# Gated MLP with ternary weights on one core: the total of |down_w| moves from TensorE to two small DMAs and VectorE, and the first eviction moves ahead of the last weights' low parts

## The reference

```python
scale = cond @ norm_w.T + 1.0
ms = jnp.mean(x * x, axis=-1, keepdims=True)
h = x * (scale[:, None, :] * jax.lax.rsqrt(ms + EPS))
u = h @ up_w.T
val, gate = jnp.split(u, 2, axis=-1)
h = val * jax.nn.gelu(gate, approximate=False)
hq = act_quant(h)
wq = weight_quant(down_w)
y = hq @ wq.T
return y + x
```

```python
scale = 1.0 / jnp.clip(jnp.mean(jnp.abs(w)), 1e-05, None)
return jnp.clip(jnp.round(w * scale), -1.0, 1.0) / scale
```

## Time and profile before

| | us |
|---|---|
| median of 3 runs | 426.77 |
| lowest, highest | 426.59, 426.85 |
| the profiled execution's own time | 426.46 |
| its span | 424.7 |
| TensorE busy in the span | 420.3 (99%) |
| VectorE busy | 279.4 (66%) |
| ScalarE busy | 187.9 (44%) |
| GpSimd busy | 165.2 (39%) |
| granted TensorE clock, mean | 1.000 |

### The profile page before, as it was taken

The page is one execution under the profiler, slowest core; times in us unless marked ns, Lnnn a source line. Parts: engine busy times, 40 slices in busy tenths (PEclk is TensorE's granted clock), DMA queues, the critical chain, the costliest instruction groups (busy, mean ns, idle before and its releaser), DMA issues.

```text
span 424.7 us, 7679 instructions
## 1 busy us (share of the span) xinstructions
PE 420.3 (99%) x2089; PEld 337.4 (79%) x2089; DVE 279.4 (66%) x538; ACT 187.9 (44%) x335; POOL 165.2 (39%) x323
## 2 busy tenths in 40 slices
PE   8999999999999999999999999999999999999997
PEld 6778888888888788888888887888888888878786
DVE  4986656756657657567566576565675565765676
ACT  6764344444344443444443444434444434444541
POOL 2644443443434434434424344334344243343320
PEclk9999999999999999999999999999999999999999
DMA  8523444333443424443334434244433344342324
GB/s 271 203 54 111 115 99 121 101 79 94 123 99 99 115 71 111 99 121 102 80 93 124 99 100 119 67 109 99 123 99 78 95 124 99 100 120 68 83 51 125
DMA packets 82088, 45.01 MB, mean 106 GB/s; under 512 B 68256, under 2 KB 68768, under 8 KB 81952
## 3 DMA queue, kind: packets, MB, share of 16 engines
q1 hardware_dynamic: 81792, 44.60, 40.3%
q10 hardware_dynamic: 288, 0.33, 0.3%
HBM read 20.00 MB, written 8.39 MB: 67 GB/s over the span
## 4 chain that ended last, share of the span: by engine, by line
PE 96%; DMA 1%; DVE 1%; ACT 1%; SPq 0%; issue 0%; POOL 0%; DVEq 0%; POOLq 0%
PE p_gate L768 41%; PE p_val L768 41%; PE p_y L788 13%; DMA up_raw<-up_w_t 1%; DVE up_lo L487 0%; PE p_val L746 0%; ACT up_hi L376 0%; DVE y_sb L531 0%; PE p_val L752 0%; PE p_val L747 0%; PE p_gate L788 0%; SPq L223 0%; ACT gelu L386 0%; DVE h L496 0%; DVE y_sb L668 0%
## 5 line engine op out<-in xcount | busy, mean ns | idle before, releaser
L625 DVE SCALAR_TENSOR_TENSOR h<-p_val,rstd,gelu 128x512 f32<-128x512 f32 x124 | 92.4, 745 | 128.0 <-PE p_val L768 127.1
L426 ACT ACTIVATE gelu<-p_gate,rstd 128x512 f32<-128x512 f32 x124 | 84.9, 685 | 142.7 <-PE p_gate L768 135.6
L299 POOL TENSOR_TENSOR mean_sq_eps<-mean_sq,rms_eps 128x1 f32<-128x1 f32 x64 | 12.2, 190 | 234.2 <-ACT squares L360 234.2
L372 ACT ACTIVATE q<-q_rounded 128x1024 bf16<-128x1024 f32 x63 | 66.6, 1057 | 77.9 <-DVE q_rounded L592 77.9
L768 PE MATMUL p_gate<-up_hi,a_lo 128*128 128x512 f32 x248 | 80.6, 406 | 0.0
L768 PE MATMUL p_val<-up_hi,a_hi 128*128 128x512 f32 x248 | 78.2, 396 | 0.0
L768 PE MATMUL p_val<-up_hi,a_lo 128*128 128x512 f32 x248 | 78.1, 396 | 0.0
L768 PE MATMUL p_val<-up_lo,a_hi 128*128 128x512 f32 x248 | 78.1, 396 | 0.0
L768 PE MATMUL p_gate<-up_hi,a_hi 128*128 128x512 f32 x248 | 78.1, 396 | 0.0
L768 PE MATMUL p_gate<-up_lo,a_hi 128*128 128x512 f32 x248 | 78.1, 395 | 0.0
L578 DVE TENSOR_REDUCE h_max<-h 128x1 f32<-128x1024 f32 x63 | 76.5, 1215 | 1.2
(11 more groups left out here) (87 smaller groups left out, 250.0 us busy)
## 6 DMA issues: line engine op xcount, KB each, us to landing
xt_in<-x_t SPq DMA_DIRECT2D x32, 256.0 KB, 2.8
x_all<-x SPq DMA_DIRECT2D x32, 256.0 KB, 2.9
out<-y_sb SPq DMA_DIRECT2D x31, 256.0 KB, 2.0
up_raw<-up_w_t SPq DMA_DIRECT2D x7, 256.0 KB, 5.3
down_raw<-down_w_t SPq DMA_DIRECT2D x1, 1024.0 KB, 7.9
q_t<-q SPq DMA_TRANSPOSE x63, 3.1
up_raw<-up_w_t ACTq DMA_DIRECT2D x1, 256.0 KB, 2.9
out<-y_sb SPq DMA_DIRECT2D x1, 128.0 KB, 2.0
```

The costliest lines, as they stand in the source:

```text
L299: pool.tensor_tensor(mean_sq_eps[:, j:j + 1], mean_sq[:, j:j + 1], rms_eps[:, :], ALU.add).then_inc(pool_step, 1)
L372: act.activation(q[j % 2][:, :], q_rounded[j % 2][:, :], ACT.Copy, bias=-ROUND).then_inc(q_ready, 1)
L426: act.activation(gelu[c][:, :], p_gate[c][:, :], ACT.Gelu, scale=rstd[:, j:j + 1]).then_inc(gelu_done, 1)
L625: nc.vector.scalar_tensor_tensor(h[s][:, c * W:(c + 1) * W], p_val[c][:, :], rstd[:, j:j + 1], gelu[c][:, :], op0=ALU.mult, op1=ALU.mult). ...
```

## The change

- The 128 sums of `abs_sum` go by a DMA into one row of one partition (`sums_row`). SyncE issues it in front of its first transpose, when ScalarE has the sums.
- VectorE adds that row up on one partition (`total`), makes a row of 128 copies times 1/(FF*D) out of it, and clips it from below (`mean_row`). These three instructions stand between the quantising of tile 0 and the last early eviction, `early_h(1, 1)`, and begin with a wait for the DMA.
- A second DMA, also ahead of SyncE's first transpose, spreads the row over the 128 partitions of `mean_abs`.
- TensorE's product with the ones goes, and so does VectorE's L504, which read its result. `ternary(0)` waits for the second DMA in its place.
- `early_h(0, 0)` on VectorE moves ahead of `low_part(3, 0)`, and `high_part(2, 1)` on ScalarE ahead of `early_gelu(0, 0)`.

```diff
+            sp.wait_ge(abs_ready, 1)
+            sp.dma_start(sums_row[0:1, :], abs_sum[:, 0:1]).then_inc(sums_in_row, 16)
+
+            sp.wait_ge(mean_in_row, 3)
+            sp.dma_start(mean_abs[:, 0:1], mean_row[0:1, :]).then_inc(mean_landed, 16)
...
             high_part(2, 0)
+            high_part(2, 1)
             early_gelu(0, 0)
-            high_part(2, 1)
             high_part(3, 0)
...
-                        act.wait_ge(ternary_step, 4)
+                        act.wait_ge(ternary_step, 3)
...
-                    dve.wait_ge(total_done, 1)
-                    nc.vector.tensor_scalar(mean_abs[:, :], p_y[1][:, 0:1], 1.0 / (FF * D), CLIP,
-                                            ALU.mult, ALU.max).then_inc(ternary_step, 1)
+                    dve.wait_ge(mean_landed, 16)
+                    nc.vector.reciprocal(down_scale[:, :], mean_abs[:, :]).then_inc(ternary_step, 1)
...
             low_part(2, 1)
+            early_h(0, 0)
             low_part(3, 0)
-            early_h(0, 0)
             low_part(3, 1)
             early_h(1, 0)
             early_h(0, 1)
             quantised(0, 0, 0)
+            dve.wait_ge(sums_in_row, 16)
+            nc.vector.tensor_reduce(total[:, :], sums_row[:, :], axis=AX.X, op=ALU.add).then_inc(mean_in_row, 1)
+
+            dve.wait_ge(consts_ready, 1)
+            dve.wait_ge(mean_in_row, 1)
+            nc.vector.tensor_scalar(mean_row[:, :], ones[0:1, :], total[:, 0:1], 1.0 / (FF * D),
+                                    ALU.mult, ALU.mult).then_inc(mean_in_row, 1)
+
+            dve.wait_ge(mean_in_row, 2)
+            nc.vector.tensor_scalar(mean_row[:, :], mean_row[:, :], CLIP, None, ALU.max).then_inc(mean_in_row, 1)
             early_h(1, 1)
             quantised(0, 1, 1)
...
-                    if first and j == TPB:
-
-                        pe.wait_ge(consts_ready, 1)
-                        pe.wait_ge(abs_ready, 1)
-                        nc.tensor.matmul(p_y[1][:, 0:1], ones[:, :], abs_sum[:, :], start=True,
-                                         stop=True).then_inc(total_done, 1)
```

More of the change, by code:

```diff
@@ L76, in build @@
         down_scale = sb("down_scale", [P, 1], fp32)
+        sums_row = sb("sums_row", [1, P], fp32)
+        mean_row = sb("mean_row", [1, P], fp32)
+        total = sb("total", [1, 1], fp32)
         x_all = sb("x_all", [P, B, TPB, D], fp32)
@@ L139, in build @@
         abs_ready = sem("abs_ready")
-        total_done = sem("total_done")
+        sums_in_row = sem("sums_in_row")
+        mean_in_row = sem("mean_in_row")
+        mean_landed = sem("mean_landed")
         ternary_step = sem("ternary_step")
@@ L501, in ternary @@
                 if stage == 0:
-                    dve.wait_ge(total_done, 1)
-                    nc.vector.tensor_scalar(mean_abs[:, :], p_y[1][:, 0:1], 1.0 / (FF * D), CLIP,
-                                            ALU.mult, ALU.max).then_inc(ternary_step, 1)
+                    dve.wait_ge(mean_landed, 16)
+                    nc.vector.reciprocal(down_scale[:, :], mean_abs[:, :]).then_inc(ternary_step, 1)
                     dve.wait_ge(ternary_step, 1)
-                    nc.vector.reciprocal(down_scale[:, :], mean_abs[:, :]).then_inc(ternary_step, 1)
-                    dve.wait_ge(ternary_step, 2)
                     nc.vector.tensor_scalar(down_tmp[:, :, :], down_raw[:, :, :], down_scale[:, 0:1], ROUND,
@@ L513, in ternary @@
                 if stage == 1:
-                    dve.wait_ge(ternary_step, 3)
+                    dve.wait_ge(ternary_step, 2)
                     nc.vector.tensor_scalar(down_tmp[:, :, :], down_tmp[:, :, :], ROUND + 1.0, ROUND - 1.0,
```

## The result

| | before | changed |
|---|---|---|
| median of 8 runs, us | 426.64 | 428.18 |
| lowest, highest | 426.57, 426.85 | 427.84, 428.40 |
| span of the profiled execution | 424.7 | 426.4 |

The ratio is 1.0034, with a 95% interval of 1.0024 to 1.0043: the change makes the kernel slower by 1.5 us. The forecast was 427.4 with a range of 426.5 to 428.2, so the time lies just inside. The sign and the place are those of the forecast; the size is not: 1.54 us came where 0.58 was summed. In the forecast's own chances the change was to stay within 0.2% with 0.68, and to be slower by more with 0.28; the less likely of the two came.

A forecast was written before the change was run, and what follows sets the result against it. TensorE, busy 99%, was taken to bound the kernel; tile 4's wait for the late gelu adds L - 0.75 - 0.35 - 0.12 = +0.58 us to 426.77, giving 427.4, range 426.5 to 428.2.

The forecast's parts named there:

- L: First DMA's time from issue to landing, taken as 1.8 us; TensorE's first product of tile 4 moves by L - 1.22.
- The early gain: TensorE up to 0.62 us earlier, from the first eviction's stall and the dropped ones product; forecast as swallowed at tile 4.
- With 0.03 each between them 0.88: VectorE's reduction, product and clip on one partition behind the first DMA: 0.28, 0.28 and 0.23 plus hops, 0.88 us.
- A rival of the prediction: The gain stands: tile 3's gelu not late, as when VectorE's later steps run faster; 426.15 to 426.7, chance 0.15.
- the slack of 0.35: Before tile 4, the margin between the end of tile 3's gelu and TensorE's weight load: 28.29 - 27.94 us.
- the credit of 0.12: At tile 4, a stopped TensorE restarts quicker: 0.34 us from freed load to second product, against 0.46 in the flow.
- The line through the two loads: A line through the 80 KB and 256 KB load times, giving 1.5 us for a DMA of no bytes.
- The rival of a slow transfer: First DMA slow: at L = 2.07 the kernel is 0.85 us slower, at L = 3.1 +1.9; chance 0.27.
- The reordering's 0.41: TensorE's stall of 0.41 us at the first eviction, waiting for the first early_h; the reordering was to remove it.
- some 0.1 of the gain is lost: If the last low part on VectorE takes as long as the slower of its kind, 0.35 us more.
- Costed at nothing: Second DMA, SyncE's first transpose, other evictions and tile 4's x: all forecast early enough to add no time.
- At most 0.62 to gain: The most the change can give: 0.41 us at the first eviction plus 0.21 from dropping the ones product.

The follow-up runs named there:

- e2: The changed kernel with both reorderings undone, so only the total by DMAs and VectorE: 428.23 us, ratio 1.0042 against the kernel before.
- e3: The changed kernel with ScalarE's conversion of the down weights moved behind the gelu of tile 3's first half: 427.42 us, ratio 1.0019 against the kernel before.
- e6: The changed kernel with the mean scaled and clipped as one 1x1 value, spread by the second DMA's repeated source: 427.58 us, ratio 1.0023 against the kernel before.
- e8: The changed kernel with an extra 128x512 reduction on VectorE behind the first DMA's wait, into an existing tile: 428.69 us, ratio 1.0045 against the kernel before.
- e4: The changed kernel with an extra 128x512 reduction on VectorE behind the first DMA's wait, into a new tile: 429.96 us, ratio 1.0079 against the kernel before.
- e7: e6 with the last early eviction ahead of VectorE's DMA wait and both DMAs on ScalarE's queue: 426.77 us against 426.69 for the kernel before, ratio 1.0002.
- e9: The kernel before with both reorderings, and GpSimd's tile 2 work held until the last low part is done: 426.40 us against 426.84, ratio 0.9994.
- e5: The kernel before with two idle 128-word DMAs in SyncE's queue, into tiles nothing reads: 426.95 us against 426.69, ratio 1.0006.
- e10: The kernel before with an unused tile of 8 bytes per partition ahead of the later buffers: 426.77 us, ratio 0.9997.

## Why the prediction was right, and where it was off

The time fell inside the range, and the chain that delays it is the one of the forecast. That it fell inside is in part luck: the range reached to 428.2 for the sake of a first DMA of up to 2.6 us, and with the 2.3 that the profile shows the forecast's own sum gives L - 1.22 = 1.08, so 427.85. The rest came from terms that it had small or not at all.

- **What bounds, and the place of the loss: right.** The gelu of tile 3, held by ScalarE's conversion, held by `ternary(1)`, stalls tile 4. e2 shows that the DMA chain alone does it, e3 that taking the conversion out of the gelu's way uncovers the next wait, e6 and e8 that the last pass follows VectorE by -0.54 for -0.54 and by +0.46 for +0.48.
- **The early gain is swallowed: right.** With and without the reordering, tile 4 begins at 29.76 and 29.80.
- **The sum: L and the three instructions behind it were mis-sized.** The eviction was forecast for 18.89 and started at 19.93, 1.04 later. Of this 0.10 is the sums' later readiness (16.25 against 16.15); 0.46 is the transfer, taken as L = 1.8 and measured with 2.3 to landing; 0.48 is the step "With 0.03 each between them 0.88", which took 1.36, because L626 took 0.80 instead of 0.28 and began 0.11 behind the reduction. Against that, L523 took 1.22 where L516 took 1.50, 0.28 less. A rival of the prediction had such a shortening for the case that GpSimd isn't beside it; GpSimd was beside it, and its a_hi was the longer one (1.70). The end of `ternary(1)` so moved by 1.05 + 1.04 - 0.28 = 1.81 (measured 1.79, 25.39 to 27.18), and less the slack of 0.35 and the credit of 0.12 this is 1.34; TensorE is 1.35 later. The slack, the credit and the 0.18 of L504 held to a hundredth or two.
- **The line through the two loads** pulled L down to 1.8. The first DMA measured 2.3 here, and in the other runs 2.0 to 2.5 and once 3.5. The rival of a slow transfer, which decided at 2.07, is the case that came, though by L alone it would have been +1.08. What I cited from the Trainium skill, DMA: Bandwidth & Descriptors, Anatomy of one DMA, 2.0 us of fixed cost, is what the second DMA with a row as its source and some of the first ones took; it was nearer than my line. What I cited from the same page of the Trainium skill, Rules for kernel authors, one descriptor per element, no run tests; with 128 elements the whole transfer took 2.0 in two of eight profiles (e4, e8), so it costs little if it holds.
- **L626 against GpSimd** was not in the prediction. In all five profiles that have this instruction (the changed kernel, e2, e3, e4 and e8) it starts at or up to 0.16 behind the start of GpSimd's a_lo and ends 0.07 or 0.08 behind its end, with 0.65 to 0.82 of length; the 1x1 instruction of e7 takes 0.14 in the middle of an a_lo. The Trainium skill, SBUF — State Buffer, SBUF: two separate sides, says that VectorE and GpSimd share a pair of ports that one instruction holds for its whole length, GpSimd's or one of VectorE's that uses both pairs. If L626 is of that kind, it waits for the end of a_lo by that rule, and the trace agrees. This is read from the ends of the rows and not shown by an edit: no run has L626 with GpSimd idle, and e4, which was to show it, did not.
- **The reordering's 0.41: the step "some 0.1 of the gain is lost" was mis-sized.** The last low part took over 1 us and was 0.33 late (the pair of 0.96 for 0.63), which left 0.08. That GpSimd does it was argued from the trace, and e9 shows it by the length of the low parts. The 0.41 itself was one execution's; e5 and e10 have 0.29 and 0.62 at the same place.
- **The tail: missing from the sum.** 0.25 are lost when SyncE's program is longer by two DMAs and their waits, at its end, 400 us later. e5 shows it with nothing else changed, and e7, with the DMAs on ScalarE, that it goes. Why SyncE issues later is open.
- **Costed at nothing: right in effect, wrong on one time.** The second DMA was issued at 20.03 and landed 2.0 later, before the reciprocal at 23.67. But the first transpose, which was to go "0.1 later or not at all", stands behind that DMA's wait and was issued at 20.69 instead of 18.92. Nothing came of it: the first down products start at 32.67, 1.35 later like the rest of TensorE's stream.
- **At most 0.62 to gain: not tested.** No run gains anything clear of noise. e9's profile lacks the stall of the first eviction, and keeps TensorE's product; no run has both of the forecast's gains and tile 4 on time.

## What to carry to other kernels

Before a small step moves from the busiest engine to others, follow the chain that waits for its result to where it touches the busy engine, and take the slack there as the budget. Here it was 0.35 us, and two transfers of 2 us with three small instructions don't fit, while the product they replaced cost 0.21. A wait put in front of an engine's queue delays everything behind it: in e7, with less to do, behind one eviction and with the DMAs on another queue, the time is that of before within a few tenths. And when an instruction on VectorE is moved, look at what GpSimd does at its new time as well as at its length at the old one.

## What the runs showed of the hardware that was not expected

- VectorE's 1x128 tensor_scalar of 0.65 to 0.82 us beside GpSimd's 128x256 subtraction, a 1x1 one of 0.14; VectorE's 128x512 subtraction over 1 us beside GpSimd's work, 0.69 without. It goes both ways: GpSimd's a_hi took 1.70 beside L523, and 0.62 at other times.
- DMAs of 128 words within SBUF: 2.0 to 3.5 us to landing for the gather into one row, 2.0 for the spread of a row, 2.5 and 3.3 with one repeated word as source.
- 0.25 us at the end of a program of 427 us from four more instructions near its start, in SyncE's queue.
- One kernel (e4) whose loop ran 0.3% slower in its profile at a granted clock of 1.00 (all five of its runs took 429.4 or more, where the delay before the loop alone makes 428.9), with one instruction and one 4-byte tile more. Neither the instruction alone (e8) nor a shift of the buffers by 8 bytes (e10) brings it back. Its cause is open.
